# An expert network walked in units of two or three tiles, with stationary up weights, in place of single tiles with stationary rows

## The reference

```python
x = x + cross_attention(layernorm(x), ctx, ctx, Wq, bq, Wk, bk, Wv, bv, We, be)
xn = layernorm(x).reshape(2048, 256)
probs = softmax(xn @ router_w + router_b)           # 8 experts
top_w, top_idx = top_k(probs, 2)
comb = sum(top_w[..., None] * one_hot(top_idx, 8), axis=1)
for e in range(8):
    h = gelu(xn @ expert_up[e].T)                    # exact, 256 -> 1024
    output += comb[:, e:e+1] * (h @ expert_down[e].T)  # 1024 -> 256
x = x + output
```

## Time and profile before

| | us |
|---|---|
| median of 3 runs | 421.69 (421.5 to 422.01) |
| span of the profiled execution | 419.6 |
| PE busy over the span | 384.8 (92%) |
| DVE busy | 239.8 (57%) |
| ACT busy | 195.7 (47%) |
| POOL busy | 164.1 (39%) |

### The profile page before, as it was taken

The page is one execution under the profiler, slowest core; times in us unless marked ns, Lnnn a source line. Parts: engine busy times, 40 slices in busy tenths (PEclk is TensorE's granted clock), DMA queues, the critical chain, the costliest instruction groups (busy, mean ns, idle before and its releaser), DMA issues.

```text
span 419.6 us, 9018 instructions
## 1 busy us (share of the span) xinstructions
PE 384.8 (92%) x2235; PEld 311.9 (74%) x2236; DVE 239.8 (57%) x690; ACT 195.7 (47%) x357; POOL 164.1 (39%) x253
## 2 busy tenths in 40 slices
PE   8889898989998889898999999999999999999960
PEld 6666675666666569896888888888888888888850
DVE  4584876899799767762327637373823643332320
ACT  3445425335434346334447747474734744443420
POOL 2324021211302121146464664555465464546441
PEclk9999999999999999999999999999999999999995
DMA  8912010400311111543227656464732222222121
GB/s 269 335 65 100 0 52 0 153 32 21 91 62 51 53 52 52 170 122 55 50 40 208 167 139 161 120 178 105 206 71 38 38 40 49 36 40 38 38 38 13
DMA packets 26388, 37.22 MB, mean 89 GB/s; under 512 B 4704, under 2 KB 17440, under 8 KB 26368
## 3 DMA queue, kind: packets, MB, share of 16 engines
q1 hardware_dynamic: 19312, 26.98, 19.3%
q0 software_dynamic: 7056, 9.99, 14.9%
HBM read 27.18 MB, written 9.79 MB: 88 GB/s over the span
## 4 chain that ended last, share of the span: by engine, by line
PE 71%; DVE 10%; DMA 5%; SPq 4%; ACT 3%; issue 3%; POOL 2%; POOLq 0%; DVEq 0%; ACTq 0%
PE bankC L1573 14%; PE bankC L1219 9%; PE bankC L1221 9%; PE bankC L1220 9%; PE bankC L1574 7%; PE bankB L1551 6%; PE bankA L1313 2%; DMA out<-xn,se 2%; PE bankA L1543 2%; PE bankB L1219 2%; PE bankB L1314 1%; DVE nmax L790 1%; PE bankC L1301 1%; DMA raw<-down 1%; DVE at_l L821 1%
## 5 line engine op out<-in xcount | busy, mean ns | idle before, releaser
L1573 PE MATMUL bankC<-dn_w,qk_h 128*128 x256 | 94.4, 407 | 1.2 <-DVE qk_l L1154 1.2
L1574 PE MATMUL bankC<-dn_w,qk_l 128*128 x256 | 71.9, 281 | 0.0
L460 POOL DMA_INDIRECT out<-x2T,idx_s x32 | 51.5, 1610 | 18.5 <-issue 18.5
L1573 PEld LDWEIGHTS bankC<-dn_w,qk_h 128*128 128x128 f32 x256 | 48.2, 188 | 11.6 <-issue 1.4
L1219 PE MATMUL bankC<-up_w,xnT_h 128*128 (+1 forms) x128 | 53.1, 415 | 1.0 <-DVE xnT_l L1148 1.0
L1161 DVE SCALAR_TENSOR_TENSOR x2T<-bankC,gate,x2T 128x256 f32<-128x256 f32 x32 | 15.4, 483 | 61.8 <-ACT x2T L682 45.5
L1221 PE MATMUL bankC<-up_w,xnT_l 128*128 (+1 forms) x128 | 50.7, 396 | 0.0
L1220 PE MATMUL bankC<-up_w,xnT_h 128*128 (+1 forms) x128 | 50.6, 395 | 0.0
L1574 PEld LDWEIGHTS bankC<-dn_w,qk_l 128*128 128x128 f32 x256 | 48.2, 188 | 0.0
L677 ACT ACTIVATE raw<-bankC 128x512 f32<-128x512 f32 x64 | 38.4, 599 | 20.3 <-PE bankC L1221 20.3
L450 POOL DMA_INDIRECT xr<-rows,idx_g x35 | 38.5, 1100 | 19.3 <-issue 19.3
(11 more groups left out here) (258 smaller groups left out, 819.0 us busy)
## 6 DMA issues: line engine op xcount, KB each, us to landing
xall<-up SPq DMA_DIRECT2D x24, 256.0 KB
xall<-down SPq DMA_DIRECT2D x24, 256.0 KB
rows<-xr SPq DMA_DIRECT2D x4, 528.0 KB
raw<-up SPq DMA_DIRECT2D x4, 512.0 KB, 4.6
raw<-down SPq DMA_DIRECT2D x4, 512.0 KB, 5.3
out<-xall SPq DMA_DIRECT2D x4, 512.0 KB, 2.8
xall<-x SPq DMA_DIRECT2D x1, 1536.0 KB, 9.6
cst<-const SPq DMA_DIRECT2D x1, 640.0 KB, 8.1
```

The costliest lines, as they stand in the source:

```text
L460: g.indirect_dma_start(out, bass.IndirectOffsetOnAxis(idx_s[:, n:n + 1], 0), y[n], None, bounds_check=T + P - 1, compute_op=ALU.add).then_ ...
L1573: mm(bankC[:, 2, :], hT_h[:, o], wd, start=(m == 0), stop=False)
L1574: last = mm(bankC[:, 2, 0:D], hT_l[:, o], wd[:, 0:D], start=False, stop=(m == KF - 1))
```

## The change

The loop's step becomes a unit of two tiles, or of three for the first unit of an expert with an odd number of tiles. An expert of n tiles has n/2 units, rounded down, and at least one. The table has a column per unit, with words for three tiles or two, the weight buffer, and the number of tiles before (`tbase_i`); its DVE chain has 40 operations where it had 26.

- **Up.** The up weights are stationary (128 x 128 blocks) and the unit's 256 or 384 rows move: 48 matmuls per unit, in four quarters of 256 rows of h each, which take turns on two pairs of PSUM banks. The product comes out with h along the partitions, as down needs it; the turns of the activation (`h_turn`) and their copies go.
- **Activation.** ACT applies GELU twice to each quarter, once rounding to the high part and once in float32 to `hbuf`; DVE takes the difference.
- **Down.** For each tile 24 matmuls of 256 columns into two banks `bankD`; high x low weights is a matmul of its own and adds into the same 256 columns. `low_part` goes; DVE scales the sum by the gate.
- **Rows.** `xr` has two rings of three tiles; a unit always gathers and turns three, and the third is not used in a unit of two.
- **Adds.** POOL's step `add(u)` copies the indices of the gathers of unit u+3, then issues adds of unit u and these gathers in turn; each add after the first waits for the landing of the one before. A unit's first result waits on DVE for the landing of all adds of unit u-2.
- **Start.** PE's first up product waits for the table. Unit 0's three gathers stand ahead of the second early add.
- **PE's code.** The weight buffer and the number of tiles are fixed in each of four bodies of a unit, for each of the two rings; a branch on the unit's word picks one.
- `den`, `at_h`, `at_l`, `y` and `hbuf` share memory with buffers of other times.

Lines that repeat are cut:

```diff
-NTAB = NT + 3
+NU = NT // 2
+NTAB = NU + 4
+TRI = 3 * P
...
+        xr = sb("xr", [P, 6, XROW])
...
+        y = [part.rearrange("p (t d) -> p t d", d=D) for part in
+             (x2T[:, :, :, :].rearrange("p t k l -> p (t k l)"), av[:, :, :].rearrange("p k l -> p (k l)"))]
...
+        bankC = ps("bankC", [P, 4, 512])
+        bankD = ps("bankD", [P, 2, 512])
+        bankB0, bankB1, bankM = bankC[:, 3, :], bankD[:, 0, :], bankD[:, 1, :]
...
+            def fetch(ring, t):
+                n = 3 * ring + t
+                g.indirect_dma_start(xr[:, n, :], None, rows, bass.IndirectOffsetOnAxis(idx_g[:, n:n + 1], 0),
                                      bounds_check=T + P - 1).then_inc(d_gather[ring], 16)
+            def give(ring, t):
+                n = 3 * ring + t
+                g.indirect_dma_start(out, bass.IndirectOffsetOnAxis(idx_s[:, n:n + 1], 0), y[ring][:, t, :], None,
                                      bounds_check=T + P - 1, compute_op=ALU.add).then_inc(d_add, 16)
...
+            def add(u, ring, nth):
+                gather_index(u + 3, 1 - ring, nth)
+                col = pool.value_load(tcol_i[:, bass.ds(u, 1)], min_val=0, max_val=MAPC - 3)
+                base = pool.value_load(tbase_i[:, bass.ds(u + 1, 1)], min_val=0, max_val=NT)
+                three = pool.value_load(w_i[:, bass.ds(u, 1)], min_val=0, max_val=4 * NE - 1) // 2 % 2
+                pool.wait_ge(d_add, 16 * base + 64)
+                g.tensor_copy(idx_s[:, 3 * ring:3 * ring + 3], slot[:, bass.ds(col, 3)]).then_inc(g_si, 1)
+                pool.wait_ge(g_si, u + 1)
+                pool.wait_ge(v_y, 2 * u + 3)
+                settle(17)
+                give(ring, 0)
+                fetch(1 - ring, 0)
+                pool.wait_ge(v_y, 2 * u + 4)
+                pool.wait_ge(d_add, 16 * base + 80)
+                settle(18)
+                give(ring, 1)
+                fetch(1 - ring, 1)
+                with pool.If(three > 0):
+                    pool.wait_ge(d_add, 16 * base + 96)
+                    settle(19)
+                    give(ring, 2)
+                fetch(1 - ring, 2)
...
             gather(0, 0, 0, col=2)
-            gather(1, 1, 0, col=3)
+            add_early(0, 1)
             pool.wait_ge(v_tab, 1)
-            nt = pool.value_load(nt_i, min_val=MINT * NE, max_val=NT)
+            nu = pool.value_load(nu_i, min_val=NE, max_val=NU)
+            gather(1, 1, 0)
+            add_early(1, 0)
             gather(2, 0, 1)
-            add_early(1, 0)
-            gather(3, 1, 1)
             add_early(1, 1)
...
+            def gelu(u, n):
+                for q in range(4):
+                    act.wait_ge(p_up, 4 * u + q + 1)
+                    bank = bankC[:, 2 * (q % 2):2 * (q % 2) + 2, 0:n * P]
+                    a.activation(hT_h[:, 2 * q:2 * q + 2, 0:n * P], bank, ACT.Gelu)
+                    a.activation(hbuf[q][:, :, 0:n * P], bank, ACT.Gelu).then_inc(a_gelu, 1)
...
+            def unit(u):
+                word = act.value_load(split_i[:, bass.ds(u, 1)], min_val=0, max_val=255)
+                sp_e, other, nraw = word // 32, 1 - word // 2 % 2, word // 4 % 8
+                with act.If(word % 2 > 0):
+                    gelu(u, 3)
+                with act.Else():
+                    gelu(u, 2)
+                x_high_f(u + 1)
                 with act.If(sp_e > 1):
+                    weights_high(other, nraw, 0)
+                    weights_high(other, nraw, 1)
...
+            def h_low(u, n):
+                for q in range(4):
+                    dve.wait_ge(a_gelu, 4 * u + q + 3)
+                    v.tensor_tensor(hT_l[:, 2 * q:2 * q + 2, 0:n * P], hbuf[q][:, :, 0:n * P],
+                                    hT_h[:, 2 * q:2 * q + 2, 0:n * P].bitcast(F32), ALU.subtract).then_inc(v_fhT, 1)
...
+            def result(ring, t):
+                return v.tensor_scalar(y[ring][:, t, :], bankD[:, (t + 1) // 2, t // 2 * D:(t // 2 + 1) * D],
+                                       gate[:, 3 * ring + t:3 * ring + t + 1], None, ALU.mult)
...
+            def unit(u, ring, nth):
+                word = dve.value_load(split_i[:, bass.ds(u, 1)], min_val=0, max_val=255)
+                done = dve.value_load(tbase_i[:, bass.ds(u, 1)], min_val=0, max_val=NT)
+                sp_e, other, three = word // 32, 1 - word // 2 % 2, word % 2
+                with dve.If(three > 0):
+                    h_low(u, 3)
+                with dve.Else():
+                    h_low(u, 2)
+                x_low_f(u + 1, 1 - ring, nth)
+                with dve.If(sp_e > 1):
+                    weights_low(sp_e, other, 0)
+                dve.wait_ge(p_dn0, u + 1)
+                dve.wait_ge(d_add, 16 * done + 64)
+                result(ring, 0).then_inc(v_y, 1)
+                with dve.If(sp_e > 1):
+                    weights_low(sp_e, other, 1)
+                dve.wait_ge(p_dn, u + 1)
+                settle(16)
+                with dve.If(three > 0):
+                    result(ring, 2)
+                result(ring, 1).then_inc(v_y, 1)
...
-            def x_turn_f(t, ring, nth):
...
+            def x_turn_f(ring, nth):
+                pe.wait_ge(d_gather[ring], 48 * (nth + 1))
+                for t in range(3):
+                    for k in range(KD):
+                        last = nc.tensor.transpose(bankA[:, k, t * P:(t + 1) * P],
+                                                   xr[:, 3 * ring + t, k * P:(k + 1) * P], ident)
                 last.then_inc(p_fxT, 1)
-            def h_turn(t):
...
-            def up_product(t, par):
...
+            def up_product(u, par, n):
+                pe.wait_ge(v_fxT, u + 1)
+                for q in range(4):
+                    pe.wait_ge(a_gelu, 4 * u + q + 1)
+                    for m in (2 * q, 2 * q + 1):
+                        w = slice(m * P, (m + 1) * P)
+                        for k in range(KD):
+                            last = three(bankC[:, 2 * (q % 2) + m % 2, 0:n * P], up_w[:, 0, par, k, w],
+                                         up_w[:, 1, par, k, w], xT_h[:, k, 0:n * P], xT_l[:, k, 0:n * P],
+                                         k == 0, k == KD - 1)
                     last.then_inc(p_up, 1)
-            def down_product(t, par):
...
+            def down_product(u, par, n):
+                pe.wait_ge(v_y, 2 * u + 2)
+                for t in range(n):
+                    out_ = bankD[:, (t + 1) // 2, t // 2 * D:(t // 2 + 1) * D]
+                    for m in range(KF):
+                        if t == 0 and m % 2 == 0:
+                            pe.wait_ge(v_fhT, 4 * u + m // 2 + 1)
+                        o = slice(t * P, (t + 1) * P)
+                        mm(out_, hT_h[:, m, o], dn_w[:, par, m, 0, :], start=(m == 0), stop=False)
+                        mm(out_, hT_h[:, m, o], dn_w[:, par, m, 1, :], start=False, stop=False)
+                        last = mm(out_, hT_l[:, m, o], dn_w[:, par, m, 0, :], start=False, stop=(m == KF - 1))
+                    if t == 0:
+                        last.then_inc(p_dn0, 1)
                 last.then_inc(p_dn, 1)
+            x_turn_f(0, 0)
             pe.wait_ge(v_pack, 1)
...
+            nc.tensor.transpose(bankM[0:8, 0:NTAB], pack[0:NTAB, :], ident[0:NTAB, 0:NTAB]).then_inc(p_tab, 1)
             pe.wait_ge(v_tab, 1)
...
-            def tile(t, ring, nth):
...
+            nu = pe.value_load(nu_i, min_val=NE, max_val=NU)
+            def body(u, ring, nth, e, par, n):
+                up_product(u, par, n)
+                x_turn_f(1 - ring, nth)
+                pe.wait_ge(v_wlo, 4 * e + 4)
+                down_product(u, par, n)
+            def unit(u, ring, nth):
+                word = pe.value_load(w_i[:, bass.ds(u, 1)], min_val=0, max_val=4 * NE - 1)
+                e, kind = word // 4, word % 4
+                pe.wait_ge(v_wlo, 4 * e + 2)
+                with pe.If(kind > 1):
+                    with pe.If(kind > 2):
+                        body(u, ring, nth, e, 1, 3)
                     with pe.Else():
+                        body(u, ring, nth, e, 0, 3)
+                with pe.Else():
+                    with pe.If(kind > 0):
+                        body(u, ring, nth, e, 1, 2)
+                    with pe.Else():
+                        body(u, ring, nth, e, 0, 2)
+            with pe.Fori(0, NU // 2) as i:
+                u = 2 * i
+                with pe.If(nu > u):
+                    unit(u, 0, i)
+                    with pe.If(nu > u + 1):
+                        unit(u + 1, 1, i + 1)
```

More of the change, by code:

```diff
@@ L486, in _ @@
[L486 removed]
+            with pool.Fori(0, NU // 2) as i:
+                u = 2 * i
+                with pool.If(nu > u):
+                    add(u, 0, i + 1)
+                    with pool.If(nu > u + 1):
+                        add(u + 1, 1, i + 2)
+            total = pool.value_load(tbase_i[:, bass.ds(nu + 1, 1)], min_val=0, max_val=NT)
+            pool.wait_ge(d_add, 16 * total + 64)
         @block.scalar
```

(35 more changed lines are left out.)

410 lines of the change are left out of this document (133 added, 277 removed).

## The result

The changed kernel takes 524.62 us (median of 4 runs, 520.21 to 524.89), before takes 421.85 (421.5 to 422.45): a ratio of 1.2409, 95% interval 1.2367 to 1.245. The prediction was 398.8 us with a range up to 412: the sign was wrong, and the range missed. In the runs beside e9 to e11, two of seven executions of before (493 and 1313 us) were in the slow state and are left out; the other five have a median of 422.21 us.

A forecast was written before the change was run, and what follows sets the result against it. The prediction took PE to bound the expert loop: -28.6 (PE's stage) + 1.0 (inside units) + 2.2 (start) + 1.0 (POOL) + 1.5 (tail) = -22.9 us, giving 398.8 us; own range 394 to 406, 8 in 10 runs 393 to 412.

The forecast's parts named there:

- rival 1: Unit heads on PE: one code block per unit waited for unhidden, 13 x 1.1 = 14 us, total 413; chance 0.13.
- PE's stage, -28.6: Expert loop on PE: seven units of 11.9 us and six of 17.5 make 188.3 us, 28.6 less than 216.9.
- The guess that no row covered: Up product in units of three tiles: matmuls of 384 columns take 0.1755 us, in proportion between 256 and 512.
- Inside the unit, +1.0 (0 to 5): Within a unit, PE's wait for activation, weight splits and DVE results: mostly covered, 1.0 us in all (0 to 5).
- Start, +2.2: Before the loop: PE's first up product waits for the longer table, near 192.0 instead of 189.82, +2.2 us.
- POOL, +1.0 (0 to 7): POOL's gathers and serial adds: 163 us in all, below PE's 188, lag just reaching later gathers, +1.0 us (0 to 7).
- Rival 2: POOL's adds: landings of 6.4 us for all would make POOL need 216 us, total 426, slower than before; chance 0.07.
- Tail, +1.5 (0.9 to 5): After the last matmul: the last unit's second add waits for the first, plus spare gathers, +1.5 us (0.9 to 5).

The follow-up runs named there:

- e9: e8, with the second and third add of a unit no longer waiting for the landing of the add before: 403.94 us, ratio to before 0.9554.
- e11: e10, with a body of its own in the odd unit for one kind (weight buffer 1, three tiles): 452.83 us, beside 422.21 for before.
- e5: Kernel before, with a branch decided at run time in each tile of the loop over 64 turns never run: 423.52 us, beside 420.4 for before.
- e1: Changed kernel with PE's 13 units written out one behind the other, no table word read, no branches: 420.34 us, beside 421.96 for before.
- e2: e1, but each unit reads its table word and passes three comparing branches that fall through: 415.52 us, beside 421.96 for before.
- e8: Changed kernel with one loop turn per unit on PE, four up products kept, turns and down product shared: 412.25 us, beside 420.4 for before.
- e10: Changed kernel with e8's shared code for the odd unit of a loop turn, four old bodies for the even: 418.1 us, beside 422.21 for before.
- e7: Kernel before, with a branch decided at run time in each tile of the loop over 512 turns never run: 429.89 us, beside 420.4 for before.

## Why the prediction was wrong

- **The step that failed:** the sum has no term for PE standing at the units' heads. It has one branch into code not yet fetched, "up to 1 us" at the start, and leaves the others to rival 1. The reason is given there: "Against it: at each tile's end PE already passes a register load, a wait and a branch, and still shows no idle time, so its sequencer runs ahead of the array". That row came from a loop of about one block, where every branch led to code that was there. (That loop holds 108 matmuls, not 92, since a down product stands behind each of its two exits; by the count of e5 it is 1.2 blocks.) It could not speak for 7.5 blocks, and the text said so and still gave the rival 0.13. In place of nothing the heads took 98.5 us. e1, e2, e8 and e10 show that this was code fetched anew.
- **Its price was mis-sized as well.** I took one block per unit at 1.1 us, the transfer of the earlier trace rows, 14 us in all. Measured: 98.5 us, 7.6 per head, since a head takes up to four blocks, mostly one behind the other, and PE stands some 3 us for each (2.7 to 3.8), not 1.1. By the early blocks that price could not be seen: they come in the order of the code, and PE shows no such wait there, as in e2.
- **A term was missing:** the clock. The loop's work without stalls is 307.2 - 89.1 = 218.0 us, against 195.9 in e8 (193.38 to 389.27): 22 us, in 11 units that run their first 3 to 6 us at 0.50.
- **The Trainium skill.** "Runtime: NRT & Kernel Launch", section "Instruction fetch mechanics", has the rule that the prediction set beside rival 1: a taken branch to a target outside the resident window waits for a fetch. The trace agrees, with 98.5 us. The same section gives PE's store as 128 KiB, and in a note says that the store is only two lines of 16 KiB. e10 runs a loop of 6.1 blocks without fetching again, which two lines exclude and the larger figure (eight such blocks) allows. e11 fetches again with its code over 6.7 blocks, which no run here explains.
- **PE's stage, -28.6:** right in kind. In e8 the loop takes 195.9 for 216.9, so -21.0. Of the 7.6 missing most lies in the units' lengths: 12.4 and 17.9 us there for 11.9 and 17.5, 6 us over 13 units. The rest is the first unit, 14.0 us (193.38 to 207.40), which runs in part at the low clock.

```profile
207.40:219.78 12.38, 12.38 (x102) 12.18 (x103) 5.27 (x10) 5.05 (x9) 7.61 (x10) 1.00 0.31 54
...
268.21:286.12 17.91, 17.91 (x127) 17.75 (x127) 10.82 (x18) 10.54 (x13) 10.22 (x13) 1.00 0.61 162
```

 The guess that no row covered, 384 columns at 0.1755 us, holds: twelve such matmuls of e8 take 0.176 each.

```profile
252.72 0.34 PE L1236 MATMUL bankC<-xnT_h,up_w 128*128 128x384 f32 x1
...
254.83 0.34 PE L1236 MATMUL bankC<-xnT_h,up_w 128*128 128x384 f32 x1
```

- **Inside the unit, +1.0 (0 to 5):** right. PE has no idle time inside units in e8: the cover held, weights and differences included.
- **Start, +2.2:** +10.6 after, with two fetches in it; 193.38 in e8, +3.6, near the end of the range given for it (194.0). The table was as forecast (its cast starts at 189.94 in e8, for 189.6); from there to the first up PE takes 3.4 us, where 2.4 had been taken.
- **POOL, +1.0 (0 to 7):** too small. The sum of POOL's units was 163 us; e8 shows some 200 (186 for twelve, and a last one), more than PE's 196. The start was later, too: POOL's first full step begins at 205.03, 11.7 us behind PE's first up, not 5. The three table words, 1.9 us a unit, I had in a lump of 2.8 that was read from a tile with one gather and one add. In the changed kernel this cost nothing, since PE was later still; it became the bound as soon as the stalls were gone, and is worth 7.5 us of span between e8 and e9. Rival 2 named the right mechanism, with a higher price than it has.
- **Tail, +1.5 (0.9 to 5):** +2.7, within its bounds.

What is not settled: at what size blocks begin to come again, whether it is the size of the loop or how its code lies in blocks (e10 against e11, e7), and by which rule the store drops a block. Whether POOL's serial adds alone would move the changed kernel was not tried.

## What to carry to other kernels

Before an inner loop is specialised into many bodies, count its code in blocks: some 127 matmuls with their loads make one here. A loop over 6.1 blocks was fetched once, one over 6.7 again in part, and one over 7.5 made PE wait at every head. Count bodies that these inputs never take, too: one of them is all that e11 adds. A wait for code has no name in the profile; look for "issue" at the head of a branch, and for instruction packets that grow with the number of turns. And when a stall is priced, add what the clock takes afterwards, and ask which engine has been hiding behind the stalled one: here the end behind PE's last matmul grew from 12.8 us before to 21 us in e8, as soon as PE was not late.

## What was not expected of the hardware

- A block costs some 3 us of idle time (2.7 to 3.8) where PE must wait for it, about three times its transfer of 1.1 us.
- A loop that spans 9.2 blocks, most of them jumped over and never run (e7), fetched eight blocks after 190 us, the last at 224, and then none. A body that is never run, among others that are (e11), brought 31 in place of 6.
- After stalls of 6 to 11 us the granted clock was 0.50 for the first 3 to 6 us of the next unit, which took 1.4 to 2.7 us more (14.9 us from 373.61 to 388.49, for 12.4).
- Adds of one unit, issued without waiting for each other, cost no more each: 1.6 us of POOL, 3.4 from one to the next at the end of e9 (389.59 to 393.01) with a gather between, against 5.7 at the end of e8 (394.74 to 400.45). Over the 19 such pairs of each run it was 3.3 to 4.9 against 4.5 to 6.6.
